# Zero-filling the dispatch buffers: three DRAM-to-DRAM copies in one batch, or seven SBUF-to-DRAM pieces in seven batches

## The chip, the cores and the metric

One NeuronCore of a Trainium2 chip runs the whole program in one launch. The metric is device time in microseconds (us) of that core. Three runs of the kernel before gave 3104.9, 3105.63 and 3107.49 us; the median, 3105.63 us, is its time. The profile is of one execution.

## The reference, cut to what matters

The program is a stack of eight layers on a tensor of 8 batches of 512 tokens with 256 features in float32. Each layer normalises its input and adds its result to it. Their order is: decay attention, experts, rotary attention, experts (the same weights), causal attention, experts with a capacity, latent attention, experts with a capacity. The first is this:

```python
q = x @ W_q;  latent_kv = (x @ W_k + x @ W_v) @ W_down_kv
k, v = latent_kv @ W_up_k, latent_kv @ W_up_v          # 16 heads of 16
scores = einsum('bhqd,bhkd->bhqk', q, k) / sqrt(256)
scores = scores * exp(-0.01 * |t - s|)
out = softmax(scores) @ v @ W_o
```

In an experts layer each token is sent to one of eight experts. The kernel does that by scattering token rows into a buffer in DRAM that is ordered by expert; every expert then reads whole tiles of 128 rows from it. Rows that no token fills are read too, so they must hold harmless values (zeros, and in the last columns a token number that lies outside the tensor) before the first experts layer scatters anything.

## The kernel before, in words

**Stages.** `prepare` loads the tokens and constants and multiplies weights together. Then `mha_layer` runs the decay attention, and after it come the experts layers (`routed_small`, `routed_large`) and the other attentions. A stage's engines run their own instruction streams, tied by semaphores; stages follow each other.

**The decay layer.** Its work is cut into 8 batches, each of 64 steps. In a step `s` TensorE (PE) makes one 128 x 512 block of transposed scores for the exponential (`exp_scores`, L1347, semaphore `b_ready`), and one block of plain scores of a later group for the row maximum (`max_scores`, L1335, `a_ready`), and every fourth step a value product (`value_sums`). ScalarE (ACT) takes the exponential (L1522); VectorE (DVE) takes the maximum times a decay table (L1605), merges the diagonal block (L1617), and at steps 4, 20, 36 and 52 splits a group's 16 maxima per row into three bf16 parts with four small instructions (`split_maxima`, L1628 to L1635: a tensor_scalar, a scalar_tensor_tensor, a cast and a tensor_tensor, each 128 x 16). PE turns these at steps 8, 24, 40 and 56 (`mT1`, `mT2`, `mT3`, `mT0` of the next batch), ACT copies them to `mT`, and two DMAs (`max_rows`, L1247) put them as three extra rows under `QS`. `exp_scores` waits for those rows at steps 16, 32, 48 and 0 of the next batch.

**Queries and keys of the next batch.** GpSimd (POOL) and ACT split each of 8 chunks of the next batch's queries and keys into three bf16 parts (L1186, L1188, L1485, L1193). SyncE (SP) writes them to a DRAM scratch with three DMAs a chunk (`write_parts`, L1226) and reads them back in the layout of the matmuls, four DMAs of 384 KB a group (`load_group`, L1239). These two and `max_rows` stand in one hand-written order on SP's queue (L1257 to L1276): group 3 of the running batch, the rows `mT1`, four chunks written, `mT2`, a chunk, group 0 of the next batch, the other three chunks, group 1, `mT3`, group 2, `mT0`.

**The clears.** `clears` (L811) makes three DMAs, one for each half's buffer `dispatched` (3072 rows of 256 floats, 3072 KB) and one for `cap_dispatched` (4096 rows of 264 floats, 4224 KB). Their source is a 128-row table of zeros in DRAM, read again for every 128-row tile. `mha_layer` gets them as `aside`; POOL issues them on its own DMA queue in the first batch at steps 32, 36 and 40 of its stream (L1768), between its splits. POOL waits for `cleared` before it scatters in an experts layer (L122, L478).

Of the kernel before, what the change touches and what calls it, by code (L numbers as in the profile page):

```python
# [8 lines left out]
F32, BF16 = mybir.dt.float32, mybir.dt.bfloat16  # L9
# [3 lines left out]
P = 128  # L13
NB, S, D = 8, 512, 256
# [25 lines left out]
ROW_W, STATS, RSTD_COL, GATE, TOKEN, TOKEN_LAST = D + 8, slice(D, D + 2), D + 2, D + 4, D + 5, D + 6  # L40
# [1 line left out]
BIG = 65536.0  # L42


CLEARS = 3
RANK_TILES = 8


# [10 lines left out]
def routed_small(nc, g, ins, results):  # L59

    X, MV, RSTD, XN, slot, weight = (g[n] for n in ("X", "MV", "RSTD", "XN", "slot", "weight"))
    ident, con, xe, ye = g["ident"], g["con"], g["xe"], g["ye"]
    RING, NQ = 8, NT // 4
    with ExitStack() as ctx:
# [16 lines left out]
        first, low3 = sb("first", [P, NT], U32), sb("low3", [P, HALF_TILES], U32)  # L81
# [36 lines left out]
        @block.gpsimd  # L118
        def _(pool):
            pool.dma_start(we[:, :, :], ins["we"]).then_inc(loaded, 16)  # L120
            pool.dma_start(be[:, :], ins["be"]).then_inc(loaded, 16)
            pool.wait_ge(g["cleared"], 16 * CLEARS)  # L122
            for h in range(2):
                pool.wait_ge(slots_ready, h + 1)
                dispatch(pool, g, XN, xe[h], range(HALF_TILES * h, HALF_TILES * h + HALF_TILES), scattered[h],
                         t_taken if h else None)
            for r in range(RING):
                pool.wait_ge(y_stored[r], 16 * (EXPERT_TILES // RING))
            for q in range(NB // 2):
                results.gather(pool, q, y_taken, EXPERT_TILES + 4 * q)  # L130
# [296 lines left out]
def routed_large(nc, g, ins, last_layer):  # L427

    X, XN, slot, rows = g["X"], g["XN"], g["slot"], g["rows"]
# [7 lines left out]
    with ExitStack() as ctx:  # L437
# [37 lines left out]

        @block.gpsimd
        def _(pool):
            pool.wait_ge(g["cleared"], 16 * CLEARS)  # L478
            for n in range(NT // GT):
                pool.wait_ge(slots_ready, n + 1)  # L480
                dispatch(pool, g, rows, g["cap_xe"], range(GT * n, GT * n + GT), scattered)
            pool.wait_ge(kept, 16 * NB)
            for e in range(E):
                for t in range(QT):
                    pool.wait_ge(y_added if last_layer else y_done, e * QT + (t + 1))
                    pool.indirect_dma_start(  # L486
                        out=to, out_offset=bass.IndirectOffsetOnAxis(ap=xin[:, e % 2, t, token:token + 1].bitcast(I32), axis=0),
                        in_=y[:, e % 2, t, 0:WIDTH], in_offset=None, bounds_check=T - 1, oob_is_err=False).then_inc(
                            sent[e % 2], 16)
# [298 lines left out]
def global_tensors(nc, ctx):  # L788

    def sb(name, shape, dt):  # L790
        return ctx.enter_context(nc.sbuf_tensor(name, shape, dt))

    rows = sb("X", [P, NT, ROW_W], F32)
    g = {"rows": rows, "X": rows[:, :, 0:D], "MV": rows[:, :, STATS],
         "RSTD": rows[:, :, RSTD_COL:RSTD_COL + 2].rearrange("p t c -> p c t"), "ids": sb("ids", [P, 2 * NT], I32),
         "ident": sb("ident_sb", [P, P], F32), "identb": sb("identb", [P, P], BF16), "eps": sb("eps", [P, 1], F32),
         "before": sb("before", [P, P], BF16), "ones": sb("ones", [P, P], BF16),
         "con_sb": sb("con_sb", [P, CON_WIDTH], F32),
         "cleared": nc.alloc_semaphore("cleared"),
         "xe": [nc.dram_tensor(f"dispatched{h}", [HALF_SLOTS, D], F32, kind="Internal").ap() for h in range(2)],  # L800
         "ye": [nc.dram_tensor(f"results{h}", [HALF_SLOTS, D], F32, kind="Internal").ap() for h in range(2)],
         "cap_xe": nc.dram_tensor("cap_dispatched", [CAP_SLOTS, ROW_W], F32, kind="Internal").ap(),
         "next_rows": nc.dram_tensor("next_rows", [T, D + 2], F32, kind="Internal").ap()}
    at, g["con"] = 0, {}
    for name, n in CON:
        g["con"][name] = g["con_sb"][:, at:at + n]
        at += n
    return g


def clears(g, zeros):  # L811

    def clear(xe):
        n, width = xe.shape[0] // P, xe.shape[1]
        return lambda eng: eng.dma_start(xe.rearrange("(a p) d -> p a d", p=P),
                                         zeros[:, 0:width].unsqueeze(1).to_broadcast([P, n, width])).then_inc(g["cleared"], 16)

    return [clear(g["xe"][0]), clear(g["xe"][1]), clear(g["cap_xe"])]


def routed_layer(nc, g, ins, capacity, last_layer=False, then=None):
# [28 lines left out]
def prepare(nc, g, w, folded):  # L850
# [9 lines left out]
    with ExitStack() as ctx:  # L860
# [20 lines left out]
        con_loaded, bns_done = sem("con_loaded"), sem("bns_done")  # L881
# [4 lines left out]
        @block.sync  # L886
        def _(sp):
            def load_tokens(batches):
                for q in batches:
                    sp.dma_start(X[:, 4 * q:4 * q + 4, :], w["x"][q]).then_inc(x_loaded[q], 16)  # L890

            for (grp, names), batches in zip(groups.items(), (range(2), range(2, 5), range(5, NB))):
                for n in names:
                    sp.dma_start(t[n][tuple(slice(None) for _ in SHAPES[n])], w[n]).then_inc(loaded[grp], 16)
                load_tokens(batches)
            sp.dma_start(g["ident"][:, :], w["ident"]).then_inc(con_loaded, 16)
            sp.dma_start(before[:, :], w["before"]).then_inc(con_loaded, 16)
            sp.dma_start(g["con_sb"][:, :], w["con"]).then_inc(con_loaded, 16)
            sp.dma_start(g["ids"][:, :], w["ids"]).then_inc(con_loaded, 16)
            for i, n in enumerate(BANKS):  # L900
                sp.wait_ge(taken, i + 1)
                sp.dma_start(folded[n].rearrange("p c d -> p (c d)"), res[:, i, :]).then_inc(stored, 16)
            sp.wait_ge(bias_done, 2)
            sp.dma_start(folded["d_kb"], kb[:, :]).then_inc(stored, 16)
            sp.wait_ge(bias_done, 4)
            sp.dma_start(folded["d_xb"], xb[:, :]).then_inc(stored, 16)
            sp.wait_ge(stored, 16 * (len(BANKS) + 2))
# [52 lines left out]
        @block.vector  # L960
        def _(dve):
            for q in range(NB):
                dve.wait_ge(x_loaded[q], 16)
                for i in range(4 * q, 4 * q + 4):
                    dve.bn_stats(st[:, i, :], X[:, i, :]).then_inc(bns_done, 1)
            dve.wait_ge(bns_done, NT)
            for i in range(NT):
                dve.bn_aggr(MV[:, i, :], st[:, i, :])
            dve.wait_ge(bias_ready, 1)
            dve.tensor_tensor(vb[:, :], psF[:, 0, 2:4], t["buv"][:, :], ALU.add).then_inc(bias_done, 1)  # L970
            dve.tensor_tensor(kb[:, :], psF[:, 0, 0:2], t["buk"][:, :], ALU.add).then_inc(bias_done, 1)
            dve.wait_ge(bias_done, 2)
            dve.tensor_copy(vbw[:, :, :], vb[:, :].unsqueeze(2).to_broadcast([P, 2, P])).then_inc(bias_done, 1)
            dve.wait_ge(xb_ready, 1)
            dve.tensor_tensor(xb[:, :], psF[:, 7, 0:D], t["bo"][:, :], ALU.add).then_inc(bias_done, 1)
            dve.wait_ge(con_loaded, 64)
            dve.tensor_copy(g["identb"][:, :], g["ident"][:, :])
            dve.tensor_copy(g["before"][:, :], before[:, :])

# [2 lines left out]
def mha_layer(nc, g, ins, decay, scale, project_q, biased, aside=(), results=None):  # L982
# [50 lines left out]
    NORMALISE_AT = 56  # L1033
    SUMS_LATER = 1 if decay else 2
    SPLIT_AT = [[SPLIT_BEFORE]] * 4
    ASIDE_FROM = 32

    A_RING = 2 if decay else 3
    A_BANK = [a % A_RING for a in range(63)] + [1]
# [47 lines left out]
    with ExitStack() as ctx:  # L1087
# [58 lines left out]
        b_ready, exp_done = sem("b_ready"), sem("exp_done")  # L1146
# [7 lines left out]
        tiles = {"wq": wq, "wk": wk, "wv": wv, "wo": wo, "tab": tab}  # L1154
# [586 lines left out]
        def _(pool):  # L1741
# [23 lines left out]

            def body(tag, b):
                for s in range(64):
                    if tag == "first" and s % 4 == 0 and ASIDE_FROM <= s < ASIDE_FROM + 4 * len(aside):  # L1768
                        aside[(s - ASIDE_FROM) // 4](pool)
                    if tag != "last":  # L1770
                        if biased and s == 4:
                            add_bias(b + 1)
                        for j in range(NCH):
                            if ROTATE_AT[j] + SUMS_LATER == s:
                                rotary_sums(pool, b + 1, j)
                                first_part(pool, b + 1, j)
                            if MIDDLE_AT[j] + 1 == s:
                                last_part(pool, b + 1, j)
# [322 lines left out]
def hybrid_stack(nc, w, out):  # L2101

    with ExitStack() as ctx:
        g = global_tensors(nc, ctx)
# [16 lines left out]
        with layer("prepare"):  # L2121
            prepare(nc, g, w, folded)
        with layer("decay"):
            mha_layer(nc, g, decay, True, 1.0 / D ** 0.5, True, False, clears(g, w["zeros"]))
        def named(name, build, *rest):
            g["layer"] = name
            build(nc, g, *rest)
# [88 lines left out]
```

## Time and profile before

| | before |
|---|---|
| time, median of 3 runs | 3105.63 us |
| the profiled execution, first to last instruction (span) | 3102.8 us |
| TensorE busy | 2629.2 us, 85% |
| VectorE busy | 1916.9 us, 62% |
| ScalarE busy | 1498.3 us, 48% |
| GpSimd busy | 784.0 us, 25% |
| SP's DMA queue (q1) | 299.42 MB, 30.9% of the 16 DMA engines' time |
| POOL's DMA queue (q0) | 49.41 MB, 4.6% |
| mean granted TensorE clock | 0.915 of full speed |

The page gives the profiled execution's span, 3102.8 us, and no separate time; what lies around the span is not in it, and the median of the runs is 2.8 us above it. Shares are averages over eight layers with different limits, so the decay layer (its scores run from 104 to 755 us) has to be read by itself. The clears are three of the 742 GpSimd instructions.

### The profile page before, as it was taken

The numbers are of one execution on the slowest core, as the hardware profiler recorded it, in microseconds if no ns is written. First come the engines' busy times: TensorE is split into PE (matmuls) and PEld (weight loads), VectorE is DVE, ScalarE is ACT, GpSimd is POOL, SyncE is SP. The second block draws the span as 40 slices with busy tenths as digits, with TensorE's granted clock in tenths as the row PEclk, the third lists the DMA queues.
The fourth block names the chain that finished last, engine by engine and source line by source line (L and its number), as shares of the span: only waits on it lengthen the run. The fifth ranks groups of instructions, "written<-read, shape, count | busy, mean of one in ns | idle before, by whom it ended". The sixth has DMA issues, their size and how long they took to land. (4 is left out here: it accounts for less than half of the span.)

```text
span 3102.8 us, 40376 instructions
## 1 busy us (share of the span) xinstructions
PE 2629.2 (85%) x12988; PEld 1365.2 (44%) x12988; DVE 1916.9 (62%) x5004; ACT 1498.3 (48%) x2912; POOL 784.0 (25%) x742
## 2 busy tenths in 40 slices
PE   4869999997576999999756797699599999985998
PEld 2324444443452333333345466466323333335666
DVE  4758888885638888888453444223488888853221
ACT  2447776776523766666642332111157776661110
POOL 0312322330233342222033211211133443304111
PEclk7789999999797999999978897799789999995999
DMA  7465555551164333223125004232433333314231
GB/s 243 152 219 165 164 165 165 165 158 35 64 201 130 103 93 113 93 83 93 46 85 184 16 1 135 82 108 99 134 103 93 97 99 113 93 45 139 83 117 54
DMA packets 216760, 351.41 MB, mean 113 GB/s; under 512 B 21465, under 2 KB 172636, under 8 KB 211816
## 3 DMA queue, kind: packets, MB, share of 16 engines
q1 hardware_dynamic: 201080, 299.42, 30.9%
q0 software_dynamic: 15472, 49.41, 4.6%
q8 instruction: 107, 1.75, 0.2%
q14 instruction: 101, 0.83, 0.1%
HBM read 199.51 MB, written 159.45 MB: 116 GB/s over the span
## 5 line engine op out<-in xcount | busy, mean ns | idle before, releaser
L1605 DVE CUSTOM_DVE_ANT_0 decay_junk<-decay_scores_q,decay_corr 128x512 bf16<-128x512 f32 x512 | 338.6, 684 | 122.8 <-PE decay_scores_q L1344 121.3
L1522 ACT ACTIVATE decay_probs<-decay_scores_k 128x512 f32<-128x512 f32 x512 | 294.7, 597 | 211.3 <-PE decay_scores_k L1363 175.0
L1608 DVE TENSOR_REDUCE rope_mx<-rope_scores_q 128x1 f32<-128x512 f32 x512 | 334.0, 685 | 89.8 <-PE rope_scores_q L1344 89.4
L1522 ACT ACTIVATE rope_probs<-rope_scores_k 128x512 f32<-128x512 f32 x512 | 294.6, 600 | 166.4 <-PE rope_scores_k L1357 165.1
L1608 DVE TENSOR_REDUCE latent_mx<-latent_scores_q 128x1 f32<-128x512 f32 x512 | 330.3, 684 | 69.6 <-PE latent_scores_q L1344 69.1
L1522 ACT ACTIVATE latent_probs<-latent_scores_k 128x512 f32<-128x512 f32 x512 | 295.0, 600 | 151.4 <-PE latent_scores_k L1357 149.5
L1344 PE MATMUL decay_scores_q<-decay_KS,decay_QS 96*128 96x512 bf16 x512 | 205.6, 402 | 47.6 <-DVE decay_mx L1605 34.7
L1344 PE MATMUL rope_scores_q<-rope_KS,rope_QS 96*128 96x512 bf16 x512 | 200.6, 394 | 21.6 <-DVE rope_mx L1608 12.3
L1344 PE MATMUL latent_scores_q<-latent_KS,latent_QS 96*128 96x512 bf16 x512 | 201.0, 395 | 21.1 <-DMA latent_QS<-latent_parts_dram 12.1
L1357 PE MATMUL latent_scores_k<-latent_QS,latent_KS 99*128 99x512 bf16 x512 | 197.2, 387 | 6.2 <-ACT latent_probs L1522 3.7
L1357 PE MATMUL rope_scores_k<-rope_QS,rope_KS 99*128 99x512 bf16 x512 | 196.6, 386 | 4.5 <-ACT rope_probs L1522 2.7
L1360 PE MATMUL decay_scores_k<-decay_QS,decay_KS 99*128 99x384 bf16 (+3 forms) x512 | 157.3, 308 | 32.6 <-DMA decay_QS<-decay_mT 25.0
L1388 PE MATMUL decay_out_heads<-decay_probs,decay_Vaug 128*32 128x512 f32 x1024 | 140.3, 620 | 0.8 <-DVE decay_probs L1617 0.8
L1186 POOL CAST decay_parts<-decay_fc 128x512 bf16<-128x512 f32 x56 | 34.2, 611 | 412.8 <-DVE decay_fc L1582 388.1
L1388 PE MATMUL latent_out_heads<-latent_probs,latent_Vaug 128*32 128x512 f32 x1024 | 136.4, 605 | 0.7 <-ACT latent_probs L1522 0.7
L1388 PE MATMUL rope_out_heads<-rope_probs,rope_Vaug 128*32 128x512 f32 x1024 | 136.4, 605 | 0.7 <-ACT rope_probs L1522 0.7
L1360 PEld LDWEIGHTS decay_scores_k<-decay_QS,decay_KS 99*128 99x128 bf16 x512 | 49.6, 97 | 193.3 <-issue 83.7
L1357 PEld LDWEIGHTS latent_scores_k<-latent_QS,latent_KS 99*128 99x128 bf16 x512 | 49.1, 97 | 182.9 <-ACT latent_probs L1522 138.5
L1357 PEld LDWEIGHTS rope_scores_k<-rope_QS,rope_KS 99*128 99x128 bf16 x512 | 49.0, 96 | 181.7 <-ACT rope_probs L1522 149.1
L204 PE MATMUL experts_logits_results<-experts_we,experts_xT 128*128 x384 | 113.1, 423 | 14.4 <-DVE experts_y L344 6.7
L54 POOL DMA_INDIRECT cap_dispatched<-X,experts_slot x64 | 63.3, 989 | 212.4 <-DVE experts_slot L718 192.9
L582 PE MATMUL experts3x_inner<-experts3x_xT,experts3x_w 128*128 128x512 f32 x256 | 113.9, 604 | 0.8 <-ACT experts3x_xT L638 0.8
(396 smaller groups left out, 5236.1 us busy)
## 6 DMA issues: line engine op xcount, KB each, us to landing
decay_parts_dram<-decay_parts SPq DMA_DIRECT2D x64, 384.0 KB, 3.0
decay_KS<-decay_parts_dram SPq DMA_DIRECT2D x64, 384.0 KB, 6.1
decay_QS<-decay_parts_dram SPq DMA_DIRECT2D x64, 384.0 KB, 6.9
decay_parts_dram<-decay_parts SPq DMA_DIRECT2D x64, 256.0 KB, 3.3
experts3x_w<-in_w_dram SPq DMA_DIRECT2D x16, 1024.0 KB, 7.3
experts4x_w<-in_w_dram SPq DMA_DIRECT2D x16, 1024.0 KB, 7.0
experts_xin<-dispatched SPq DMA_DIRECT2D x96, 128.0 KB
results<-experts_y SPq DMA_DIRECT2D x96, 128.0 KB
```

The costliest lines, as they stand in the source:

```text
L54: pool.indirect_dma_start(out=xe, out_offset=bass.IndirectOffsetOnAxis(ap=g["slot"][:, i:i + 1], axis=0), in_=rows[:, i, :], in_offset=Non ...
L204: last = pe.matmul(psL[:, n % 2, 0:D], xT[:, n % 2, c, :], we[:, c, bass.ds(at, D)], start=(c == 0), stop=(c == 1))
L582: last = pe.matmul(psH[:, f % 2, :], w1[:, p, c, f * P:(f + 1) * P], xT[:, p, c, :], start=(c == 0), stop=(c == 1))
L1186: eng.tensor_copy(parts[:, (nb * NCH + j) % RING, 0, :], fc[:, j % 2, :]).then_inc(p0_done, 1)
L1344: pe.matmul(psA[:, A_BANK[k], :], QS[0:96, 0, c, hh, qt * P:(qt + 1) * P], KS[0:96, NV - 1, c, hh, :], start=True, stop=True).then_inc(a_r ...
L1357: last = pe.matmul(psB[:, s % 2, :], KS[:, 0, c, hh, keys], QS[:, 0, c, hh, :], start=True, stop=True)
L1360: last = pe.matmul(psB[:, s % 2, 0:end], KS[:, 1, c, hh, keys], QS[:, 0, c, hh, 0:end], start=True, stop=True)
L1388: last = pe.matmul(psO[32 * h:32 * h + 32, :], Vaug[:, b % 2, kt, 4 * grp + h, :], probs[:, (b * 16 + kk) % PSLOTS, h, :], start=(kt == 0) ...
L1522: act.activation(probs[:, (b * 16 + kk) % PSLOTS, h, :], psB[:, s % 2, :], ACT.Exp, scale=scale).then_inc(exp_done, 1)
L1605: dve.tensor_tensor_reduce(junk[:, a % 2, :], psA[:, A_BANK[k], :], corr[:, qt, :], 1.0, -3.0e38, ALU.mult, ALU.max, mx[:, grp % 2, qt, h: ...
L1608: dve.tensor_reduce(mx[:, grp % 2, qt, h:h + 1], psA[:, A_BANK[k], :], AX.X, ALU.max).then_inc(a_done, 1)
```

## The change

Three things are changed. `prepare` loads the table of zeros (128 x 264 floats, 132 KB) into a new SBUF tile `blank`, as a fifth constant behind the others, and DVE waits for all five before it converts the constants. The zeros are written from that tile, in pieces of at most 12 tiles of 128 rows: 12 and 12 for each `dispatched`, and 12, 12 and 8 for `cap_dispatched`: seven pieces, six of 1536 rows and one of 1024. And POOL issues piece `b` in batch `b` (0 to 6) at step 5 of its stream, after waiting until PE has finished the scores of step 4 of that batch. The waits for `cleared` count seven DMAs and not three.

```diff
-CLEARS = 3
+CLEAR_TILES = 12
...
-            pool.wait_ge(g["cleared"], 16 * CLEARS)
+            pool.wait_ge(g["cleared"], 16 * g["clears"])
...
+         "blank": sb("blank", [P, ROW_W], F32), "cleared": nc.alloc_semaphore("cleared"),
...
-    def clear(xe):
-        n, width = xe.shape[0] // P, xe.shape[1]
-        return lambda eng: eng.dma_start(xe.rearrange("(a p) d -> p a d", p=P),
-                                         zeros[:, 0:width].unsqueeze(1).to_broadcast([P, n, width])).then_inc(g["cleared"], 16)
-    return [clear(g["xe"][0]), clear(g["xe"][1]), clear(g["cap_xe"])]
+    def clear(xe, first, n):
+        rows = xe[first * P:(first + n) * P, :].rearrange("(a p) d -> p a d", p=P)
+        return lambda eng: eng.dma_start(rows, g["blank"][:, 0:xe.shape[1]].unsqueeze(1).to_broadcast(
+            [P, n, xe.shape[1]])).then_inc(g["cleared"], 16)
+    made = []
+    for xe in (*g["xe"], g["cap_xe"]):
+        tiles = xe.shape[0] // P
+        made += [clear(xe, a, min(CLEAR_TILES, tiles - a)) for a in range(0, tiles, CLEAR_TILES)]
+    g["clears"] = len(made)
+    return made
...
+            sp.dma_start(g["blank"][:, :], w["zeros"]).then_inc(con_loaded, 16)
...
-            dve.wait_ge(con_loaded, 64)
+            dve.wait_ge(con_loaded, 80)
...
-                    if tag == "first" and s % 4 == 0 and ASIDE_FROM <= s < ASIDE_FROM + 4 * len(aside):
-                        aside[(s - ASIDE_FROM) // 4](pool)
+                    if s == ASIDE_AT and b < len(aside):        # ASIDE_AT = 5
+                        pool.wait_ge(b_ready, b * 64 + ASIDE_AT)
+                        aside[b](pool)
```

## Rows read from the trace of the kernel before

**Rows 1.** The page, part 2: busy tenths of PE and of DMA in 40 slices.
```profile
PE   4869999997576999999756797699599999985998
...
DMA  7465555551164333223125004232433333314231
```

**Rows 2.** Waits of PE, 100 to 208 us, then 287 to 367: total, times, longest.
```profile
PE decay_scores_k L1360 <- DMA decay_QS<-decay_mT: 25.0, 1, 25.0
PE decay_scores_q L1344 <- DVE decay_mx L1605: 3.3, 12, 0.8
```

**Rows 3.** Busy time by stretch: PE, PEld, DVE, ACT, POOL, PEclk, DMA share, GB/s.
```profile
170.00:175.00 5.00, 0.00 (x0) 0.00 (x0) 0.00 (x0) 0.00 (x0) 0.00 (x0) 0.90 1.04 338
195.00:200.00 5.00, 5.00 (x24) 1.99 (x24) 3.23 (x9) 2.88 (x5) 0.00 (x0) 0.50 0.67 254
```

**Rows 4.** Timeline of SP, DMAs of the maxima's rows: start us, us, instruction, tiles.
```profile
142.15 1.47 SPq L1247 DMA_DIRECT2D decay_QS<-decay_mT  x2
228.17 1.48 SPq L1247 DMA_DIRECT2D decay_QS<-decay_mT  x2
248.80 1.47 SPq L1247 DMA_DIRECT2D decay_QS<-decay_mT  x2
307.62 1.47 SPq L1247 DMA_DIRECT2D decay_QS<-decay_mT  x2
...
466.54 1.48 SPq L1247 DMA_DIRECT2D decay_QS<-decay_mT  x2
548.57 1.47 SPq L1247 DMA_DIRECT2D decay_QS<-decay_mT  x2
```

**Rows 5.** DMA, 145 to 215 us, then 160 to 170, then all of POOL's: KB, us to landing.
```profile
q0 software_dynamic: 2608, 10.62, 44.1%
...
decay_QS<-decay_parts_dram SPq DMA_DIRECT2D x2, 384.0 KB, 25.6
...
experts_we<-in_we_dram POOLq DMA_DIRECT2D x2, 2048.0 KB, 8.3
```

**Rows 6.** Timeline of POOL, DVE and PE around the second and third clear.
```profile
154.96 1.45 POOL L815 DMA_DIRECT2D dispatched<-in_zeros_dram  x1
155.55 0.85 DVE L1628 TENSOR_SCALAR decay_mp<-decay_mx 128x16 bf16<-128x16 f32 x1
156.65 1.42 DVE L1633 CAST decay_mp<-decay_mr 128x16 bf16<-128x16 f32 x1
158.97 0.40 PE L1373 MATMUL decay_scores_q<-decay_QS,decay_KS 99*128 99x128 bf16 x4 [2.23 <-DVE decay_probs L1617]
```

**Rows 7.** Timeline of PE and DVE at steps 4 to 7 of batch 2.
```profile
299.71 0.27 PE L1363 MATMUL decay_scores_k<-decay_QS,decay_KS 99*128 99x256 bf16 x1
300.86 0.17 DVE L1628 TENSOR_SCALAR decay_mp<-decay_mx 128x16 bf16<-128x16 f32 x1
...
302.19 0.67 DVE L1605 CUSTOM_DVE_ANT_0 decay_junk<-decay_scores_q,decay_corr 128x512 bf16<-128x512 f32 x1
...
303.94 0.38 PE L1344 MATMUL decay_scores_q<-decay_KS,decay_QS 96*128 96x512 bf16 x1
```

**Rows 8.** Batch 1: two stretches (columns of Rows 3), and ACT at step 16.
```profile
220.00:229.00 9.00, 8.82 (x57) 4.33 (x53) 7.89 (x21) 6.85 (x13) 3.48 (x4) 1.00 0.01 2
235.00:239.00 4.00, 4.00 (x25) 1.90 (x17) 2.56 (x8) 2.94 (x6) 1.71 (x3) 1.00 1.01 342
...
236.11 0.60 ACT L1522 ACTIVATE decay_probs<-decay_scores_k 128x512 f32<-128x512 f32 x1 [0.22 <-PE decay_scores_k L1363]
```

**Rows 9.** POOL's DMA instructions by line: ns least/median/most, starts.
```profile
L815 POOL DMA_DIRECT2D dispatched<-in_zeros_dram x2: 1450/1546/1641, 151.1 to 155.0; - x2
L54 POOL DMA_INDIRECT dispatched<-experts_XN,experts_slot x64: 972/976/1056, 813.3 to 1635.4; - x64
```

**Rows 10.** `prepare`: DVE's conversion of a constant, and a stretch (columns of Rows 3).
```profile
30.40 0.22 DVE L977 CAST identb<-ident_sb 128x128 bf16<-128x128 f32 x1
...
27.00:33.00 6.00, 2.07 (x4) 1.17 (x4) 1.55 (x13) 0.00 (x0) 0.00 (x0) 0.50 0.20 68
```

More of the change, by code:

```diff
@@ L477, in _ @@
         def _(pool):
-            pool.wait_ge(g["cleared"], 16 * CLEARS)
+            pool.wait_ge(g["cleared"], 16 * g["clears"])
             for n in range(NT // GT):
@@ L798, in global_tensors @@
          "con_sb": sb("con_sb", [P, CON_WIDTH], F32),
-         "cleared": nc.alloc_semaphore("cleared"),
+         "blank": sb("blank", [P, ROW_W], F32), "cleared": nc.alloc_semaphore("cleared"),
          "xe": [nc.dram_tensor(f"dispatched{h}", [HALF_SLOTS, D], F32, kind="Internal").ap() for h in range(2)],
@@ L808, in global_tensors, with clears @@
     return g
-def clears(g, zeros):
-    def clear(xe):
-        n, width = xe.shape[0] // P, xe.shape[1]
-        return lambda eng: eng.dma_start(xe.rearrange("(a p) d -> p a d", p=P),
-                                         zeros[:, 0:width].unsqueeze(1).to_broadcast([P, n, width])).then_inc(g["cleared"], 16)
-    return [clear(g["xe"][0]), clear(g["xe"][1]), clear(g["cap_xe"])]
+def clears(g):
+    def clear(xe, first, n):
[8 more added lines that the diff above has]
+    return made
 def routed_layer(nc, g, ins, capacity, last_layer=False, then=None):
@@ L1035, in mha_layer @@
     SPLIT_AT = [[SPLIT_BEFORE]] * 4
-    ASIDE_FROM = 32
+    ASIDE_AT = 5
     A_RING = 2 if decay else 3
@@ L2123, in hybrid_stack @@
         with layer("decay"):
-            mha_layer(nc, g, decay, True, 1.0 / D ** 0.5, True, False, clears(g, w["zeros"]))
+            mha_layer(nc, g, decay, True, 1.0 / D ** 0.5, True, False, clears(g))
         def named(name, build, *rest):
```

## The prediction

> **What bounds the kernel now.** I read the page's slices first, to see where the engine that carries the kernel is held up. In the decay layer PE's digit is 9 in slices 4 to 9, but 6 in the third (155 to 233 us), where DMA has 6 against 5 in those behind it [rows 1]. So the layer runs at PE's pace except in one place. The waits of PE name it: one wait of 25.0 us for the DMA of the rows of maxima, against nothing longer than 0.8 us in a whole later batch [rows 2]. The stretches show what it looks like: at 170 to 175 us no compute engine does anything while the 16 DMA engines are full (1.04 of their time, 338 GB/s), and when PE restarts at 195 it does so at a granted clock of 0.50, the 1.2 GHz level [rows 3]. The DMA view says who fills them: the clears on POOL's queue, 10.62 MB, take 44.1% of 70 us. The queue column reads packets, MB, share. A 384 KB load of SP's issued among them takes 25.6 us to land [rows 5]. The 12 KB rows stand behind such loads on SP's queue. The clears are therefore what holds the layer, not their bytes as such but that all of them come inside 5 us, where SP also has to write and read its chunks.
>
> **What removing them from the first batch gives.** From the rows of `mT2` in batch 0 to those of `mT1` in batch 1 there are 228.17 - 142.15 = 86.02 us. The same stretch of the program one batch later takes 307.62 - 248.80 = 58.82 us [rows 4]. Both begin before a clear is issued (151 us) or where none is, and both do the same work on every engine. The excess is 27.20 us. It holds the 25.0 us of waiting, PE's slow clock after it, and the 2.23 us that PE stood for DVE around the second and third clear [rows 6]. Batch 0 without clears should run like batch 1, because SP's traffic is the same in both; so the first term is **-27.2 us**. What is late next is nothing: batch 1 has PE waits of 3.3 us in all for DVE, and these are in both kernels.
>
> **What the pieces' data cost.** A piece is 1536 rows, 1.57 MB (1.62 MB in the wide buffer). As q0 took 44.1% of 70 us for 10.62 MB, it moved them at 10.62 / 30.9 = 344 GB/s of full engines [rows 5]; stores from SBUF in rows of 1 KB go at 342 GB/s [rows 8]. Either gives 4.6 to 4.7 us a piece. In batch 1 the release comes at about 220.6 us (batch 2's, 299.98, less the 79.45 between 307.62 and 228.17) [rows 4, 7]. A 2048 KB load of POOL's lands 8.3 us after its issue [rows 5], 2.2 us more than its 6.1 us at that rate, so a piece should land about 7 us after 220.6, near 228. From 220 to 229 us the DMA engines are 0.01 busy [rows 8]. The next user is the pair of row DMAs at 228.17, and what needs them is step 16, whose exponential starts at 236.11 [rows 4, 8]. In 7.9 us they can wait out whatever is left of the piece. SP's chunk writes fill the engines only from about 235 (1.01) [rows 8]. I take **0**. From below it is 0 as well, since nothing runs that could be sped up; from above, a row DMA that had to wait for a whole piece from its own issue on would still land about 5 + 2 us later and be in time, so the bound is 0 to 1 us a piece, 7 us.
>
> **What the pieces' issue costs.** POOL is held while it makes the descriptors: 1.45 to 1.64 us for 3072 rows [rows 9]. Half the rows should take more than half of that and less than the whole; I take 1.0 us, with 0.7 and 1.7 as ends. POOL has nothing else there; its first split of the batch waits for DVE's product at step 6. But DVE can be held. During the second clear (154.96 to 156.41) the tensor_scalar of 128 x 16 took 0.85 us where it has 0.17, ending at 156.40, and during the third the cast took 1.42 us [rows 6, 7]. A piece released at 299.71 + 0.27 = 299.98 is issued until about 301.0, and DVE's tensor_scalar of the same kind starts at 300.86 [rows 7]. So it would lose 0.15 us, and 0.8 us if the issue took 1.7. PE needs nothing of DVE that comes after it before 303.94: its matmul there waits for the maximum that DVE ends at 302.86, which leaves 1.08 us of slack [rows 7]. Even the upper end is inside this. I take **0** for PE, seven times.
>
> The Trainium skill, page "SBUF — State Buffer", section "Who interferes with whom", has a rule for this: DVE's copies, casts and tensor_scalars in a two-port mode and GpSimd lock each other out for a whole instruction, and a tensor_tensor does not stop descriptor generation. The trace agrees for the first part (the tensor_scalar 0.85 us against 0.17). By the rule alone every piece meets one cast or tensor_scalar, and how much it costs is the overlap, so the sum above stays.
>
> What the small shift can do is to move DVE against POOL later in the batch. There the same four instructions meet POOL's splits. In batch 4 it cost most, and the batch took 548.57 - 466.54 = 82.03 us against 79.45 [rows 4]: 2.6 us for one such meeting. After, it may vanish (-2.6) or come in every batch with a piece (7 x 2.6 = 18). The value nearest to the rows is that such meetings stay about as rare as they are; I add **+0.5** for the seven small shifts.
>
> **What `prepare` pays.** One more load of 132 KB behind the constants is 0.4 us of the DMA engines, and one more issue on SP is 0.47 us like its neighbours. DVE wants it at 30.40 us, when the engines have been nearly idle since 27 (0.20 from 27 to 33) [rows 10]. The last store of `prepare` waits for DVE, not for the queue. Bounds 0 and 0.9 us; I take **+0.5**. The counts of `cleared` cost nothing: the last piece lands near 220.6 + 5 x 79.45 + 10 = 628 us and the first scatter is at 813 us [rows 9].
>
> **Sum.** -27.2 + 0 + 0 + 0.5 + 0.5 = -26.2 us. The profiled span of 3102.8 becomes 3076.6; the median of the runs stands 2.8 us above the span, so the time is 3105.6 - 26.2 = **3079.4 us**. From the bounds: -27.2 - 2.6 = -29.8 gives 3075.8, and -27.2 + 7 + 18 + 0.9 = -1.3 gives 3104.3, which needs all of it at once.
>
> **Rivals.** (a) The meetings of POOL and DVE become common. For it: they hang on tenths of a microsecond, and every piece shifts DVE a little. Against: at step 5 the slack takes the first delay. Four more of them cost 10.4 us: 3089.8. (b) The stall is partly SP's own. For it: SP's chunks alone fill the DMA engines (1.01 of them at 235 us) [rows 8]. Against: they do so in each batch, and the later one shows no DMA wait of PE [rows 2]. If half of the 25.0 us stayed: 3091.9. (c) Slower: the issue holds DVE long. Were a row from SBUF as dear as a row of an indirect DMA, 976 ns for 128 rows or 7.6 ns a row [rows 9], a piece would hold POOL 11.7 us, and DVE's tensor_scalar until the end. The slack is used up at an issue of 0.88 + 1.08 = 1.96 us; each microsecond beyond it stops PE. Seven times 11.7 - 1.96 is 68 us, less 27.2: 3147. It turns from gain to loss at 1.96 + 27.2 / 7 = 5.8 us an issue, 3.8 ns a row. Against it: a clear cost 0.5 ns a row, and that it reads DRAM and not SBUF is no reason for eight times as many nanoseconds. (d) The new kernel still bunches its zeros: if `b_ready` let POOL pass early, all would pile up at the layer's start. Against: the wait is for an absolute count, and a batch has 64. It would give back the stall in another place: 3105.
>
> **Chances.** Forecast 0.78, (a) 0.12, (b) 0.05, (c) 0.03, (d) 0.02. What a measurement can tell from no change is about 0.2%, 6.2 us. Faster by more than that (under 3099.4): forecast, (a) and (b), 0.95; within it: (d), 0.02; slower: (c), 0.03. The range takes the lower bound less 1.8 us of run-to-run scatter and goes up to four extra meetings and as little: 3074 to 3091.
>
> **What would show it.** After: no PE wait on `decay_QS<-decay_mT` above 1 us. The stretch from `mT2` of batch 0 to `mT1` of batch 1 near 58.8 us. Seven POOL DMA instructions of about 1.0 us, each landing in 7 to 10 us, one 79.45 us after the other. The tensor_scalar L1628 of each batch's step 4 up to 0.3 us longer. No slow clock from 174 to 201 us. I am wrong if an issue takes over 2 us, if PE waits at step 7 of the batches, or if the row DMAs of `mT1` land after step 16.

## The result, and the profile after

The changed kernel took **3076.03 us** (median of 4 runs, 3075.45 to 3080.01) against 3106.56 us (3104.9 to 3110.33, 4 runs) for the kernel before on the same chip: a ratio of **0.9899, with an interval of 0.9885 to 0.9914**, or 27 to 36 us less. The profiled span went from 3102.8 to 3074.2 us, by 28.6.

The page, part 2, of the changed kernel, which answers to [rows 1]:

```profile
PE   4799999997677999999766797799599999976998
...
DMA  7565556541353332322135004232432333213231
```

The 6 in PE's third slice is a 9. DMA has 6 there in both; what the engines moved in that slice fell from 219 to 191 GB/s. The waits of PE from 100 to 664 us (total, times, longest) say the same:

```profile
PE decay_scores_q L1350 <- DVE decay_mx L1611: 20.5, 75, 0.8
PE decay_scores_q L1379 <- DVE decay_probs L1623: 10.3, 15, 2.0
PE decay_work L1312 <- ACT decay_xnT L1463: 7.9, 7, 1.1
PE decay_scores_q L1350 <- DMA decay_QS<-decay_parts_dram: 0.5, 1, 0.5
```

The 25.0 us for `decay_QS<-decay_mT` of [rows 2] are gone, and what is left for a DMA is 0.5 us in seven batches. Next, SP's timeline of the maxima's rows, for [rows 4]: `mT2` of batch 0, `mT1` and `mT2` of batch 1, `mT1` of batch 2.

```profile
140.71 1.47 SPq L1253 DMA_DIRECT2D decay_QS<-decay_mT  x2
196.80 1.47 SPq L1253 DMA_DIRECT2D decay_QS<-decay_mT  x2
216.84 1.47 SPq L1253 DMA_DIRECT2D decay_QS<-decay_mT  x2
275.68 1.47 SPq L1253 DMA_DIRECT2D decay_QS<-decay_mT  x2
```

The stretch that took 86.02 us takes 196.80 - 140.71 = 56.09, and the same stretch one batch on 58.84. From `mT1` to `mT1` there are 275.68 - 196.80 = 78.88 us, where a batch of the kernel before had 79.45. The last view is the busy time in stretches (columns of [rows 3]): these two, then the 5 us in which nothing ran.

```profile
140.71:196.80 56.09, 51.36 (x332) 21.91 (x331) 45.51 (x133) 40.10 (x76) 11.29 (x13) 1.00 0.68 199
216.84:275.68 58.84, 54.07 (x347) 25.10 (x347) 49.28 (x145) 40.26 (x76) 11.35 (x13) 1.00 0.65 190
...
170.00:175.00 5.00, 4.51 (x33) 1.80 (x31) 4.55 (x16) 3.44 (x7) 0.00 (x0) 1.00 0.27 70
```

At 170 us PE works at a granted clock of 1.00, and the DMA engines, full before, are 0.27 busy. There is no stretch at 0.50 behind a stall, because there is no stall. The two first rows also hold what the prediction did not see: PE has 332 matmuls in the one and 347 in the other.

**Where the 28.6 us are.** The start of a batch is its first exponential. Batch by batch from 0 to 6, the kernel before took 110.26, 79.45, 79.45, 79.47, 82.03, 79.47 and 80.58 us; the changed one 78.39, 78.87, 80.42, 78.89, 81.46, 80.11 and 81.40. So the account is: start of the layer +0.5, batch 0 -31.9, batches 1 to 6 +0.7 together, the last batch and the layer's end +1.6, all layers behind it +0.5. Batch 0 is more than the whole gain. Its 31.9 are 29.9 in the stretch above (86.02 - 56.09), and 1.9 ahead of it: from the batch's first exponential to the first row above there are 36.03 us and were 37.97, as PE's granted clock rose from 0.50 to 1.00 at 107.8 us and not at 112.6.

### The profile page after: what moved, and what is told of

The parts are those of the page before. It is cut to its first block and busy times, and to the rows that moved or that the text cites. A ratio compares the mean times of both kernels' runs of the same rounds, so it can differ in the third digit from the quotient of the medians.

```text
span 3074.2 us, 40382 instructions
## 1 busy us (share of the span) xinstructions
PE 2631.1 (86%) x12988; PEld 1367.2 (44%) x12988; DVE 1911.7 (62%) x5004; ACT 1500.8 (49%) x2912; POOL 789.0 (26%) x746
## 5 line engine op out<-in xcount | busy, mean ns | idle before, releaser
L1350 PE MATMUL decay_scores_q<-decay_KS,decay_QS 96*128 96x512 bf16 x512 | 204.2, 400 | 45.8 <-DVE decay_mx L1611 33.5
L582 PE MATMUL experts3x_inner<-experts3x_xT,experts3x_w 128*128 128x512 f32 x256 | 113.9, 604 | 0.8 <-ACT experts3x_xT L638 0.8
L582 PE MATMUL experts4x_inner<-experts4x_xT,experts4x_w 128*128 128x512 f32 x256 | 113.1, 600 | 0.8 <-ACT experts4x_xT L638 0.8
```

The source lines that it names most:

```text
L582: last = pe.matmul(psH[:, f % 2, :], w1[:, p, c, f * P:(f + 1) * P], xT[:, p, c, :], start=(c == 0), stop=(c == 1))
L1350: pe.matmul(psA[:, A_BANK[k], :], QS[0:96, 0, c, hh, qt * P:(qt + 1) * P], KS[0:96, NV - 1, c, hh, :], start=True, stop=True).then_inc(a_r ...
```

## The experiments

Four chips were used. The kernel before had medians of 3106.6, 3109.9 (E1 to E4), 3076.2 (E5 to E8) and 3073.2 us (E9 to E11) on them, so a time is compared only through its ratio to the runs beside it. In the profiled executions the layers behind the decay layer took 2335 us (changed kernel), 2342 to 2345 (E1 to E4) and 2302 to 2310 (E5 to E11). The decay layer itself is comparable across them: a quiet batch without a piece took 79.4 to 79.5 us on all four chips (batch 6 also 79.1). All diffs are against the changed kernel and cut to what matters; E1, E3, E6 and E7 also take out the three lines that issue a piece at `ASIDE_AT`, and these are not shown. The times that E2 to E4 were expected to take had been set by the first chip, and they miss them: 3084 us against 3074 to 3081. The decay layer ended where it did in the changed kernel (738.4 to 739.8 us against 739.1), and the missing microseconds are behind it, where E1 has them too.

**E1, the source alone: three whole clears from SBUF, at the old steps.**

```diff
-CLEAR_TILES = 12
+CLEAR_TILES = 32
...
+                    if aside and tag == "first" and s in (32, 36, 40):
+                        aside[(s - 32) // 4](pool)
```

> The source alone: the changed kernel's SBUF source, but three whole clears at steps 32, 36 and 40 of the first batch, as before. Theory (what held PE was that all zeros stood in the DMA engines at once): zeros from SBUF take the engines as long as from DRAM (342 against 344 GB/s), so the wait of PE for the rows of maxima stays between 20 and 28 us, and the time is within 3 us of before, 3106. Rival (the DRAM reads of the zeros were the burden: 10.6 MB read beside 10.6 MB written): the wait falls under 10 us and the time under 3090.

Measured: 3110.65 us (10 runs), ratio 1.0002 [0.9991, 1.0013]. Batch 0 took 108.6 us. The waits of PE, 100 to 260 us:

```profile
PE decay_scores_k L1366 <- DMA decay_QS<-decay_mT: 23.5, 1, 23.5
```

The stall of [rows 2] stands, 23.5 us for 25.0, though no zero is read from DRAM any more, and the stretch from `mT2` of batch 0 to `mT1` of batch 1 takes 86.21 us for 86.02. What batch 0 is shorter by (108.6 for 110.3) lies ahead of that stretch, where the clock rose earlier. The SBUF tile by itself gives nothing.

**E2, the spreading alone: the seven pieces copied from the table in DRAM.**

```diff
-        return lambda eng: eng.dma_start(rows, g["blank"][:, 0:xe.shape[1]]...
+        return lambda eng: eng.dma_start(rows, zeros[:, 0:xe.shape[1]]...
```

> The spreading alone: the seven pieces at step 5 of their batches, read from the DRAM table. Theory: like the changed kernel, no PE wait for the rows over 1 us, time 3076 within 2 us. Rival (the source matters): part of the gain is lost, over 3082, with pieces that land in more than 8 us against 6.9.

Measured: 3084.23 us, ratio 0.9911 [0.988, 0.9943]. Batch 0 took 77.6 us, a quiet batch 78.9. Behind the first, an issue of 12 tiles took 1.01 to 1.04 us (the changed kernel's 1.04 to 1.08), and a piece landed after 7.7 us (median; the changed kernel's after 6.9). The time can't be told from the changed kernel's: the gain is the spreading.

**E3, place: no piece before the last batch.** All seven are issued in batch 7, where SP writes no chunks.

```diff
+                    if aside and tag == "last" and s in (8, 12, 16, 24, 28, 32, 40):
+                        pool.wait_ge(b_ready, b * 64 + s)
+                        aside[(8, 12, 16, 24, 28, 32, 40).index(s)](pool)
```

> No zeros in batches 0 to 6: all seven pieces go out in batch 7, at steps 8, 12, 16, 24, 28, 32 and 40, where SP moves nothing but the rows of maxima. It shows what batches 0 to 6 are without any zeros. Theory: batch 0 takes 78.4 us as in the changed kernel, because a batch 0 without stall is shorter than batch 1 by the missing output projection of a batch before it (so the gain is 31.9 us against the old batch 0 and not 27.2). The quiet ones of batches 1 to 6 take 79.45 us as before the change, since the 0.58 us that they gained come from the piece delaying DVE by 0.32 us; so the time is 3076 to 3081. Rival (the pieces cost something small in each batch): quiet batches at or under 78.87 us, and the time under 3075.

Measured: 3084.02 us, ratio 0.9914 [0.9892, 0.9935]. Batch 0 took 78.5 us with no zeros in it at all, as with one piece (78.4): a piece at step 5 costs the batch nothing that shows. In all executions without bunched zeros, leaving out E5 with its pieces at step 20, batch 0 took 77.1 to 79.0 us, so a cost of under about 1 us would not show. But the quiet batches are back at 79.5, as these two rows of SP (`mT1` of batches 2 and 3) show, 79.50 us apart:

```profile
277.77 1.47 SPq L1253 DMA_DIRECT2D decay_QS<-decay_mT  x2
357.27 1.47 SPq L1253 DMA_DIRECT2D decay_QS<-decay_mT  x2
```

**E4, who issues: the pieces on SP's queue, at the start of each batch.**

```diff
+                if b < len(aside):
+                    sp.wait_ge(b_ready, b * 64 + 1)
+                    aside[b](sp)
...
-                    if s == ASIDE_AT and b < len(aside):
-                        pool.wait_ge(b_ready, b * 64 + ASIDE_AT)
-                        aside[b](pool)
```

> The same seven pieces, issued by SP right behind the load of group 3 in each batch and not by POOL, so no descriptors are made by GpSimd. Theory: the tensor_scalar of step 4 is back at 0.17 us (0.49 with POOL's piece in batch 1), the product of step 8 is held again (1.6 us against 0.69), quiet batches are back at 79.45 us, no PE wait for a DMA; time 3076 to 3081. Rival (the 0.58 us come from somewhere else, as from the DMA queue): quiet batches stay at 78.87 us and the time is 3074 to 3076. Second rival (the rows of maxima now stand behind the piece on one queue): PE waits for them at step 16 of the batches, over 1 us each, time above 3083.

Measured: 3083.98 us, ratio 0.9917 [0.9892, 0.9942]. An issue holds SP 0.38 us, a piece lands after 11.2 us (median), and PE waits for no DMA. Quiet batches took 79.5 us, with the data moved and POOL left alone. So the 0.58 us that the changed kernel's quiet batches are shorter come from POOL's issue, not from the zeros' transfer.

What the issue does is seen at step 8 of batch 1. First DVE and POOL in the changed kernel (timeline: start, us, engine, instruction):

```profile
189.49 1.08 POOL L815 DMA_DIRECT2D dispatched<-blank  x1 [37.01 <-PE decay_scores_k L1369]
190.04 0.49 DVE L1634 TENSOR_SCALAR decay_mp<-decay_mx 128x16 bf16<-128x16 f32 x1
194.16 0.69 DVE L1588 TENSOR_TENSOR decay_fc<-decay_f,decay_tab 128x512 f32<-128x512 f32 x1
194.36 1.51 POOL L1194 TENSOR_TENSOR decay_rr<-decay_fc,decay_parts 128x512 f32<-128x512 f32 x1
```

Then the same in E4:

```profile
190.10 0.17 DVE L1637 TENSOR_SCALAR decay_mp<-decay_mx 128x16 bf16<-128x16 f32 x1
194.14 1.16 POOL L1194 TENSOR_TENSOR decay_rr<-decay_fc,decay_parts 128x512 f32<-128x512 f32 x1
194.22 1.62 DVE L1591 TENSOR_TENSOR decay_fc<-decay_f,decay_tab 128x512 f32<-128x512 f32 x1
```

And in the kernel before:

```profile
225.45 1.16 POOL L1188 TENSOR_TENSOR decay_rr<-decay_fc,decay_parts 128x512 f32<-128x512 f32 x1
225.53 1.62 DVE L1582 TENSOR_TENSOR decay_fc<-decay_f,decay_tab 128x512 f32<-128x512 f32 x1
```

In both of these POOL's TENSOR_TENSOR starts first, by 0.08 us, and DVE's product beside it lasts 1.62 us. In the changed kernel POOL's issue stretches the tensor_scalar by 0.49 - 0.17 = 0.32 us; four microseconds later the order is turned round, DVE's product lasts 0.69, and it is POOL's that is long (1.51 for 1.16). The Trainium skill, page "SBUF — State Buffer", section "Who interferes with whom", says that a DVE instruction with two SBUF inputs and a GpSimd one that reads SBUF contend, and that the order of issue decides which of them blocks. The trace agrees: with starts only 0.08 and 0.20 us apart, the engine that started first was the short one.

**E7, that race alone: E3 with a DVE copy of 0.29 us at step 4 of every batch, its result unused.**

```diff
+                        if aside and s == 4:
+                            if b:
+                                dve.wait_ge(pad_done, b)
+                            dve.tensor_copy(pad[:, :], corr[:, 0, 0:256]).then_inc(pad_done, 1)
```

> The 0.58 us of the quiet batches by itself: the kernel with all pieces in batch 7, and in each batch a copy of 128 x 256 floats to an unused tile on DVE ahead of the four small instructions at step 4. Nothing of POOL's or of the DMA engines is changed in batches 0 to 6; DVE is only some 0.3 us late. Theory: DVE's product of step 8 then starts ahead of or behind POOL's tensor_tensor in the other order, is not held 1.6 us any more, and quiet batches take 78.9 us against 79.45 with all pieces in batch 7 alone. Rival (the gain came from the zeros' place): they stay at 79.45 us or more.

Measured: 3050.22 us (beside a kernel before of 3076.2), ratio 0.992 [0.9903, 0.9938]. Batch 1, no piece near:

```profile
189.33 0.29 DVE L1729 COPY decay_pad<-decay_corr 128x256 f32<-128x256 f32 x1
193.45 0.69 DVE L1590 TENSOR_TENSOR decay_fc<-decay_f,decay_tab 128x512 f32<-128x512 f32 x1
193.53 1.62 POOL L1196 TENSOR_TENSOR decay_rr<-decay_fc,decay_parts 128x512 f32<-128x512 f32 x1
...
196.09 1.47 SPq L1255 DMA_DIRECT2D decay_QS<-decay_mT  x2
274.97 1.47 SPq L1255 DMA_DIRECT2D decay_QS<-decay_mT  x2
```

Useless work of 0.29 us a batch on DVE turns the race, and the batch takes 78.88 us, the changed kernel's to the digit, for E3's 79.50. In the ratio it is too small to see: six such batches are 3.5 us, about 0.1%, and batches 1 to 6 together took 482.2 us for E3's 483.4. The traces of the other runs agree. In every batch from 1 to 6 of the kernel before and of E1, E3, E4, E5 and E6 the product of step 8 lasts 1.62 to 1.63 us, and in every one of the changed kernel, of E7, E8 and E10 it lasts 0.69. E11 (below) has both in one execution: 0.69 us and batches of 78.9 us where a piece is issued, 1.62 and 79.5 in its quiet batch without one. The one odd batch is E2's batch 6, with the smaller piece, where it lasts 1.68.

**E5, the step: pieces at step 20 and not 5.** Step 20 has a split of maxima too, and SP's chunk writes go on beside it.

```diff
-    ASIDE_AT = 5
+    ASIDE_AT = 20
```

> The place in the batch: the changed kernel, each piece at step 20 and not 5. There DVE splits the maxima of group 2 while GpSimd already has its own splits, and SP's chunk writes fill the DMA engines. Theory (step 5 is cheap because the DMA engines and DVE have room there): DVE is held longer, PE waits for the diagonal merge 1 to 2 us in most batches and its clock falls after it, 1.5 to 2.6 us in most of seven batches; time 3084 to 3098 against 3076 to 3084 for the changed kernel on one chip. Rival (any place will do, once the zeros are spread): within 2 us of the changed kernel.

Measured: 3066.95 us beside 3076.2, ratio 0.9971 [0.9956, 0.9986]. Two thirds of the gain are gone: batches 0 to 6 took 80.6 to 84.4 us. That is more than the 1.5 to 2.6 us a batch that were expected. Batch 1, timeline of POOL, DVE and PE, and the stretch behind it:

```profile
214.53 1.06 POOL L815 DMA_DIRECT2D dispatched<-blank  x1
214.86 1.95 DVE L1639 CAST decay_mp<-decay_mr 128x16 bf16<-128x16 f32 x1
217.72 0.40 PE L1379 MATMUL decay_scores_q<-decay_QS,decay_KS 99*128 99x128 bf16 x4 [2.70 <-DVE decay_probs L1623]
...
218.00:221.00 3.00, 2.82 (x13) 0.44 (x12) 2.65 (x9) 0.58 (x1) 1.76 (x2) 0.55 0.99 337
```

The cast (0.17 us by itself) lasts 1.95: the issue holds it to 215.59, and POOL's TENSOR_TENSOR from 215.61 to 216.78 directly behind takes it over. In batches 1, 2, 3, 5 and 6 it lasts 1.79 to 1.95. In the changed kernel POOL is idle at this place for 0.52 us (211.02 to 211.54), and the cast runs in that gap (from 211.29, 0.18 us); here the issue fills the gap. PE stands for 2.70 us, and its granted clock then is 0.55. PE's waits for DVE's merge come to 21.4 us in the layer, to 10.7 in the changed kernel. The DMA engines are not what costs: the pieces landed after 5.4 to 7.3 us, and PE waited 0.3 us in all for a load of `QS`. By the traces it is not the issue's microsecond alone that costs, but that at step 20 a split stands right behind it; at step 5 POOL has three microseconds free.

**E6, how thin is thin enough: seven pieces in batch 0, one every 8 steps.**

```diff
+                    if aside and tag == "first" and s % 8 == 5 and s // 8 < len(aside):
+                        pool.wait_ge(b_ready, s)
+                        aside[s // 8](pool)
```

> Cut but not spread over batches: all seven pieces in batch 0, one every 8 steps from step 5 on. Theory (PE stops only when the zeros stand in front of SP's loads at the steps 32 to 48; the engines have 38 of 78 us free in a batch without zeros, and the pieces need 32): the wait for the rows of maxima falls from 25.0 to under 8 us, batch 0 takes 80 to 88 us against 110.3 before and 78.4 in the changed kernel. Rival (a batch can't carry all zeros however they are cut): over 15 us of DMA waits, batch 0 over 95 us.

Measured: 3063.52 us beside 3076.2, ratio 0.9954 [0.9939, 0.997]; batch 0 took 96.4 us. The waits of PE, 100 to 202 us:

```profile
PE decay_scores_k L1366 <- DMA decay_QS<-decay_mT: 10.5, 2, 9.9
PE decay_scores_k L1366 <- ACT decay_probs L1528: 3.4, 1, 3.4
PE decay_scores_q L1350 <- DMA decay_QS<-decay_parts_dram: 1.9, 1, 1.9
```

The waiting lies between the two expectations, the batch's time in the rival's. Of the 25 us of waiting for DMA 12.4 remain, and ACT's 3.4 come on top. ACT is late for the same reason: it stood 3.61 us for POOL's split, and that had stood 5.50 us for a chunk write to land (timelines of POOL and ACT):

```profile
149.93 0.61 POOL L1192 CAST decay_parts<-decay_fc 128x512 bf16<-128x512 f32 x1 [5.50 <-DMA decay_parts_dram<-decay_parts]
151.80 0.62 ACT L1491 CAST decay_parts<-decay_rr 128x512 bf16<-128x512 f32 x1 [3.61 <-POOL decay_rr L1194]
```

The pieces were not evenly spaced either. They were issued at 113.9, 125.3, 138.8, 152.8, 157.9, 168.9 and 188.7 us, the fourth and the fifth 5.1 us apart, since POOL was behind with its splits. The fourth to the sixth landed after 12.0 to 12.5 us, in the same stretch as SP's chunks. So the run shows that seven pieces fitted in like this are too many for batch 0; how far apart they would have to be it doesn't show.

**E11, the size: four pieces, of 24, 24, 24 and 8 tiles, in batches 0 to 3.**

```diff
-CLEAR_TILES = 12
+CLEAR_TILES = 24
```

> How large a piece step 5 can carry: 24 tiles, so four pieces (24, 24, 24 and 8 tiles) in batches 0 to 3. The data of one take 9.4 us of the engines and the issue about 1.5 us. Theory (7.9 us of slack for the rows of maxima, 1.08 us for DVE): no PE wait for a DMA over 1 us; the tensor_scalar is held to 0.7 to 1.0 us; ratio to before 0.989 to 0.991, as the changed kernel. Rival (12 tiles is near the limit): PE waits for the rows at step 16 or the chunk writes push the loads out, over 2 us in each of batches 0 to 2, ratio over 0.992.

Measured: 3047.21 us beside 3073.2, ratio 0.9907 [0.9888, 0.9926]. POOL's DMA instructions by line (ns, starts):

```profile
L815 POOL DMA_DIRECT2D dispatched<-blank x2: 1474/1558/1642, 110.4 to 189.0; - x2
...
DMA to landing us min/median/max: 5.5/13.3/14.2
```

A whole half of the buffer at once, 3.1 MB, lands after 13.0 to 14.2 us and stops no one: PE's longest wait for a DMA to 345 us is 0.2. The tensor_scalar of step 4 was held to 0.89 and 0.84 us in batches 1 and 2, as expected, and the batches still took 78.9. Twelve tiles are not a threshold; the gap in the DMA engines' work behind step 5 takes 24 as well.

**E9, one of the meetings taken out: DVE's splits of maxima one step later.**

```diff
-    SPAN, SPLIT_BEFORE = (-28, -13), -12
+    SPAN, SPLIT_BEFORE = (-28, -13), -11 if decay else -12
```

> A version meant to beat both. The changed kernel with the four small instructions of DVE one step later in each group (steps 5, 21, 37 and 53), so that they fall elsewhere against GpSimd's splits, above all at step 20, where the tensor_scalar is held to 0.9 us in quiet batches and where batches of 80 to 83 us lose 1.5 to 4 us with a slow clock behind it. Theory (those meetings are what is left above 78.87 us a batch): fewer of batches 1 to 6 are above 79.5 us, up to 8 us in all; ratio to before 0.987 to 0.990. Rival (they meet as often one step later, or the maps' rows come too late for step 8): ratio 0.990 to 0.995.

Measured: 3045.8 us beside 3073.2, ratio 0.9897 [0.9876, 0.9918], the changed kernel's. The waits for the merge, 10.7 us in the layer, went, and those for the maxima came in their place: 33.5 us for 21.4 of E8, in waits no longer than 1.2. Quiet batches took 79.7 us. DVE's delay was handed on to another wait. The shift also turned the race of step 8 back: the product lasts 1.68 us in all of batches 1 to 6, where the kernel before has 1.62. So this version took out one meeting and brought back the other.

**E10, the load in `prepare` taken out: POOL fills `blank` with memsets.**

```diff
-            sp.dma_start(g["blank"][:, :], w["zeros"]).then_inc(con_loaded, 16)
...
+            pool.memset(g["blank"][:, 0:TOKEN], 0.0)
+            pool.memset(g["blank"][:, TOKEN:ROW_W].bitcast(I32), NO_TOKEN)
...
-            dve.wait_ge(con_loaded, 80)
+            dve.wait_ge(con_loaded, 64)
```

> The changed kernel with the zeros tile filled by two memsets on GpSimd at the start and not loaded: it takes away the load that the prediction priced at 0.5 us. Theory: the first decay exponential starts 0.5 us earlier (104.2 against 104.7 us), nothing else is moved. Rival (the load is hidden, and the 0.5 us are scatter): it starts at 104.7 to 105.5 as in the changed kernel's two profiles.

Measured: 3041.27 us beside 3073.2, ratio 0.9887 [0.9867, 0.9907]. It can't be told from the changed kernel. The first exponential of the decay layer starts at 105.05 us without the load; with it at 104.68 in the first and at 105.47 in the second run of the same changed kernel. E1 and E4, which have the load, start at 104.2 like the kernel before, E11 at 103.7. The load costs nothing that shows.

**E8, the changed kernel again,** beside E5 to E7.

> The changed kernel once more, unaltered, on the same chip as its variants, since the layers behind the decay layer took 7 to 10 us more in the four variants than in its own profile. Theory (that is the chip's and not the variants'): the decay layer ends at 738 to 740 us, and the rest takes as long as in the runs beside it; ratio to before 0.990 to 0.992. Rival (the variants cost something behind the decay layer): the rest takes 2335 us here and 2342 or more in those beside it.

Measured: 3045.57 us beside 3076.2, ratio 0.9896 [0.988, 0.9913]. The ratio holds on a chip where both kernels are 30 us faster. The decay layer ended at 737.8 us, and the layers behind it took 2306 us, as in E5 to E7 (2302 to 2307): their length is the chip's and not the variants'. Batch 4 took 81.0 us and batch 5 81.7, where the first run had 81.5 and 80.1: how long a batch is changes from one execution to the next.

## Why the prediction was right, and where it was off

3079.4 us were forecast, faster by 26.2; measured were 3076.03, inside the range, and a gain of 30.5 between the medians, 27 to 36 with its interval. The forecast gain lies just under that interval, and the term that was too small is named below.

**What bounds the kernel: right.** The stall was the bunching of the zeros in batch 0, as E1 (bunched, from SBUF: stall) and E2 (spread, from DRAM: none) show from both sides. Rival (b), a stall partly SP's own, falls with the 0.5 us of DMA waits in the changed kernel; rival (d), zeros still bunched, with the starts of the pieces below, 111.8 to 589.2 us. One reading of [rows 2] was too good: in a quiet batch of the kernel before PE also waits once 1.1 us for ACT (`decay_xnT`) and 1.1 us in two waits for DVE's merge, the longer 0.9, so nothing longer than 0.8 holds for the row that was shown alone, and the waits for DVE are 4.4 us and not 3.3. Both kernels have them, and the sum doesn't change.

**"Both do the same work on every engine": wrong.** This was the step behind the term of -27.2, which measured -29.9. Batch 1 computes output projections of the batch before it; batch 0 has none. The traces of both kernels have 16 matmuls `decay_work<-decay_wo,decay_attnT` in batch 1's stretch and none in batch 0's, and DVE has 12 instructions for the layer's result in the one alone. The two rows of stretches show the sum of it: 51.36 us of matmuls in batch 0's, 54.07 in batch 1's, 15 fewer. So batch 0 without a stall should be shorter by 2.7 us than the 58.82 of batch 1, and it is by 2.75 in the changed kernel (56.09 against 58.84). A count of PE's matmuls in the two stretches of the kernel before, 331 against 346, would have shown it.

**The pieces' data, at 0: right.** A piece landed 5.1 to 7.2 us after its issue, under the 7 to 10 expected. E3 and E4 show from both sides that batch 0 is as long with the data as without (78.5 and 79.0 us), within the scatter of batch 0 told at E3.

**The pieces' issue, at 0 for PE: right, and its size nearly.** POOL's DMA instructions by line in the changed kernel (ns, starts):

```profile
L815 POOL DMA_DIRECT2D dispatched<-blank x4: 1039/1058/1240, 111.8 to 348.8; - x4
L815 POOL DMA_DIRECT2D cap_dispatched<-blank x3: 905/1039/1039, 427.7 to 589.2; - x3
```

1.04 to 1.08 us where 1.0 was taken, 0.90 for eight tiles. The first, 1.24 us, is no guide to the rest. The tensor_scalar loses 0.32 us in batch 1, at the edge of "up to 0.3", 0.27 in batches 2 to 5 and 0.14 in batch 6, and PE nothing at step 7. Rival (c), 11.7 us an issue, is dead.

**The small shifts, at +0.5: the sum is near (+0.7), the mechanism was two of opposite sign.** The prediction had only the meetings of POOL and DVE that can stop PE, and gave them 0.5. The shift also turned a meeting that every batch has, at step 8, and this gained 0.58 us in quiet batches (E3, E4 and E7 show it). More long batches than before (80.42, 80.11 and 81.40 where 79.45, 79.47 and 80.58 were) ate it. These are no meetings. At step 20 of batch 2 DVE's four instructions last as long as in batch 1, but the stretches there (columns of [rows 3]), first of batch 1 and then of batch 2, differ in the granted clock:

```profile
211.00:213.00 2.00, 0.89 (x10) 0.43 (x7) 1.90 (x8) 1.64 (x4) 1.19 (x2) 1.00 0.75 253
213.00:215.00 2.00, 2.00 (x16) 0.60 (x16) 1.97 (x7) 0.63 (x2) 1.14 (x2) 1.00 0.72 239
290.00:292.00 2.00, 0.88 (x8) 0.36 (x6) 1.93 (x7) 1.62 (x4) 1.17 (x1) 1.00 0.67 229
292.00:294.00 2.00, 2.00 (x9) 0.20 (x8) 1.97 (x7) 0.29 (x1) 1.47 (x2) 0.52 0.75 253
```

PE pauses for 1.1 us in both; behind it the clock stays at 1.00 in the one and falls to 0.52 in the other (0.50 is the 1.2 GHz level), whose exponentials are 1.5 us late from step 26 on. Batch 5 loses 1.2 us like this at step 44 (0.58 from 558 to 560 us), and batch 6 of the kernel before lost 1.5 at step 20 (0.52 from 645 to 647 us). Why the clock falls in one batch and not in the next is open: it changed between two executions of the same kernel. The meeting that [rows 4] priced at 2.6 us is batch 4's, where the cast of step 20 lasts 1.02 us. It is there in every execution but E9's. In E8, whose clock stayed at 1.00 behind it, it cost 1.1 us; the other 1.5 of the 2.6 are the clock's, which stood at 0.58 from 484 to 488 us in the kernel before. Rival (a), meetings in every batch, is what E5 makes of it: step 20 has it, step 5 has not.

**`prepare`, at +0.5: the number came out, the cause did not.** The layer starts 0.5 us later, but E10 without the load starts within the spread of two runs with it. As far as these runs can tell it is scatter, and the term should have been 0.

**Not in the sum:** the last batch with the layer's end, +1.6 us, and the clock's earlier rise in batch 0, -1.9. Neither belongs to the change as far as the runs show. The same changed kernel in E8 took 73.3 us from the start of batch 7 to the layer's end, as the kernel before did, where its first run took 74.8. E1, whose decay layer is unchanged until 149 us, and E10, which doesn't load the tile in `prepare`, also have a clock of 1.00 from 110 to 115 us, where the kernel before had 0.74. Of the kernel before there is one profile, so how often its clock rises that late is not known.

With the first term at its true size the sum is -28.9, for a span that moved by -28.6. That the two agree so well is partly luck, since 1.9 and 1.6 cancel.

## What to carry to other kernels

A background transfer is priced by what waits behind it on the same 16 engines, not by its bytes: the same 10.6 MB cost 28 us in one burst and nothing that shows in seven parts, each with a gap behind it in which nobody needs a DMA soon. The place is chosen by two gaps at once, one in the DMA engines' work and one in the issuing engine's own stream, and the second decided as much (step 5 against step 20). When a stage is priced by its undisturbed twin, count the instructions of both first.

## What the runs showed of the hardware

- A DRAM-to-DRAM copy that reads one 128-row table over and over and a store of the same zeros from SBUF are nearly alike: an issue of 1.01 to 1.04 against 1.04 to 1.08 us, landing after 7.7 against 6.9, and bunched a stall of 25.0 against 23.5 us in a stretch of 86.02 against 86.21.
- POOL's issue time doesn't follow the size in proportion: 0.90 us for 8 tiles of 128 rows, 1.04 to 1.08 for 12, 1.44 to 1.48 for 24 and 1.70 for 32; the first of a kernel is longer, 1.24 for 12 and 1.64 for 24. A piece of 12 holds SP 0.38 us (E4).
- A delay of 0.3 us on one engine can speed up the kernel: two instructions of DVE and POOL that start 0.08 to 0.20 us apart lengthen one of the two by 0.35 to 0.93 us, and which one it is decides 0.58 us of a batch.
- After the same pause of PE, 1.1 us, the granted clock stayed at 1.00 in batch 1 and fell to 0.52 in batch 2 of one execution; the fall cost 1.5 us.
- The same program differed by 1% from chip to chip (3073 to 3110 us for the kernel before), as much as the whole effect measured here. By the profiles of the variants nearly all of it is behind the decay layer; the ratio held (0.9899 and 0.9896, each known to about 0.0015).
